# Softmax pass's node stage of a graph network: early gathers of run ends, no mask product, one product moved to the second node stage

## The reference

```python
# layer 0: softmax aggregation          N = 6250 nodes, E = 100000 edges
m = relu(feat[src]) + 1e-7
ex = exp(m - segment_max(m, dst)[dst])
msg = segment_sum(ex / segment_sum(ex, dst)[dst] * m, dst)
x = layernorm(x + (x + msg) @ W + b)
# layer 1: messages over edges (mlp: relu(h @ W + b), then normalised over all rows)
node_feat = mlp(x, W_node, ...); edge_feat = mlp(edge_attr, W_edge, ...)
message = mlp(concat([x[src], x[dst], edge_feat]), W_msg, ...)
x = layernorm(x + segment_sum(message, dst) + node_feat)
# layers 2 and 3: two mean-aggregating convolutions each, relu or elu between
```

## Time and profile before

| | us |
|---|---|
| time, median of 3 runs | 4437.25 (4429.48 to 4437.64) |
| profiled execution, span | 5171.8 |
| PE busy in it | 3159.9 (61%) |
| DVE busy | 2679.3 (52%) |
| POOL busy | 2510.8 (49%) |
| ACT busy | 1560.3 (30%) |

### The profile page before, as it was taken

One profiled execution on the slowest core, in us unless ns is written; L12 is line 12 of the kernel. 1 busy time (PEld: TensorE's weight loads), 2 busy tenths in 40 slices (PEclk: granted clock), 3 DMA queues, 4 the chain that ended last, 5 costly groups with the idle time before them and its releaser, 6 DMA issues.

```text
span 5171.8 us, 61853 instructions
## 1 busy us (share of the span) xinstructions
PE 3159.9 (61%) x18737; PEld 2317.1 (45%) x18737; DVE 2679.3 (52%) x5868; ACT 1560.3 (30%) x3684; POOL 2510.8 (49%) x2587
## 2 busy tenths in 40 slices
PE   1555555554755555555555554111159999999999
PEld 0333333333534344344344333100047777788777
DVE  4888888888645555555555556300001254433333
ACT  1777777776222222222222222100000011111000
POOL 7666666664666666666666666777720000000000
PEclk9999999999986667667667666555579999999999
DMA  5555555555134444444444443100037666666776
GB/s 183 192 198 191 195 194 194 192 192 164 56 98 111 112 121 111 116 117 111 114 118 112 111 118 85 58 0 0 13 126 282 215 218 245 247 248 251 259 276 228
DMA packets 387596, 797.88 MB, mean 154 GB/s; under 512 B 207412, under 2 KB 264600, under 8 KB 361128
## 3 DMA queue, kind: packets, MB, share of 16 engines
q1 hardware_dynamic: 239330, 586.35, 33.9%
q0 software_dynamic: 82320, 90.28, 7.9%
q10 hardware_dynamic: 65718, 118.62, 6.2%
HBM read 581.03 MB, written 213.92 MB: 154 GB/s over the span
## 4 chain that ended last, share of the span: by engine, by line
PE 25%; issue 23%; SPq 19%; DVE 3%; another core or an unknown queue 1%; DMA 0%; ACTq 0%; ACT 0%; DVEq 0%; POOL 0%
PE ps L1181 18%; SPq L626 14%; PE ps L1111 6%; SPq L601 1%; SPq L596 1%; SPq L622 1%; SPq L607 1%; SPq L617 1%; PE ps L1064 1%; ACTq L64 0%; DMA area<-adj 0%; PE ps L1083 0%; PE ps L1056 0%; DVE second L1650 0%
## 5 line engine op out<-in xcount | busy, mean ns | idle before, releaser
L770 POOL DMA_INDIRECT area<-src_table,early x784 | 752.5, 960 | 469.6 <-remote 225.5
L770 POOL DMA_INDIRECT area<-relu_table,early x784 | 739.6, 943 | 421.3 <-issue 212.4
L953 PE MATMUL ps<-ident,area 96*128 96x96 f32 x2352 | 441.4, 356 | 804.3 <-issue 555.4
L953 PEld LDWEIGHTS ps<-ident,area 96*128 96x128 f32 x2352 | 355.2, 213 | 939.2 <-issue 782.4
L1181 PE MATMUL ps<-second,area 128*128 128x288 bf16 x5194 | 652.1, 286 | 0.2 <-DVE second L1823 0.2
L1682 DVE TENSOR_TENSOR_SCAN area<-flags,area,ps 96x512 f32<-96x512 int8 x196 | 250.0, 1276 | 647.6 <-issue 552.0
L1181 PEld LDWEIGHTS ps<-second,area 128*128 128x128 f16 x5194 | 509.0, 98 | 128.5 <-DVE second L1823 0.5
L1650 DVE SCALAR_TENSOR_TENSOR second<-second,area,ps 128x512 bf16<-128x512 f32 x784 | 538.1, 741 | 0.0
L857 POOL DMA_INDIRECT adj<-out_ring x390 | 395.5, 1014 | 127.8 <-issue 127.8
L781 POOL DMA_INDIRECT adj<-copies_ring,cell_ring x392 | 388.6, 991 | 125.6 <-issue 118.9
L1111 PE MATMUL ps<-early,area 128*128 128x288 bf16 x2401 | 322.0, 292 | 204.9 <-issue 204.9
(11 more groups left out here) (330 smaller groups left out, 4709.0 us busy)
## 6 DMA issues: line engine op xcount, KB each, us to landing
area<-adj SPq DMA_DIRECT2D x147, 1632.0 KB
area<-adj SPq DMA_DIRECT2D x55, 1568.0 KB
adj<-early SPq DMA_DIRECT2D x102, 816.0 KB
soft_sums<-out_ring ACTq DMA_DIRECT2D x196, 384.0 KB
second<-key_dram SPq DMA_DIRECT2D x98, 512.0 KB
area<-dst_table SPq DMA_DIRECT2D x784, 48.0 KB
sums<-out_ring ACTq DMA_DIRECT2D x196, 192.0 KB
second<-caps_dram SPq DMA_DIRECT2D x98, 192.0 KB
```

The source lines that it names most:

```text
L770: pool.indirect_dma_start(out=src_rows[:, s, c, :], out_offset=None, in_=gather_table[p], in_offset=bass.IndirectOffsetOnAxis(ap=src_cols[ ...
L953: last = nc.tensor.transpose(ps[:, b, c * F:(c + 1) * F], r[:, (s * CH + c) * P:(s * CH + c + 1) * P], ident[0:F, 0:F])
```

## The change

POOL gathers run ends of groups 0 to 4 (FIRST_ENDS = 5, as many as fit in `area` behind the rings of the edge pass) right after its last gather of `relu_table`. Each of these groups waits for `first_ends_stored`, which SP signals after its last load of the softmax pass, when as many rounds of sums are stored as `group_stored` names for the group. Groups 5 and 6 are gathered after the last sums. Neither mask product is left: `end_row` of a node without edges now points at an extra row behind `soft_sums` and `sums`, and the product with `has` goes from POOL's L825 and from `join` (L1800). SP writes those rows, and zeros over the last three rounds of `soft_sums` (12 stores), before its wait for `later_stored`.

PE's steps in the softmax node stage are taken apart and put in another order; W_node's product, its Relu and Square move into the message node stage, ahead of the joins. `node_feat` holds the turned result in the meantime. The buffer of destination rows becomes five. DVE's `cells_of_edges`, and with it PE's turns and SP's stores of keys, move behind the node stage. Coefficients and constants of the message pass move ahead of DVE's and ACT's wait for the tables, and POOL waits for `src_table` alone. The loops over groups are written out.

The diff, cut to its core:

```diff
+        RINGS_END = RING * CH * F + 2 * RING * TE
+        FIRST_ENDS = (area.shape[1] - RINGS_END) // (GT * 2 * F)
+        def soft_ends(g):
+            at = RINGS_END + g * GT * 2 * F if g < FIRST_ENDS else (g - FIRST_ENDS) * GT * 2 * F
+            return area[:, at:at + GT * 2 * F].rearrange("p (k f) -> p k f", f=2 * F)
...
# SP, setup
+            sp.dma_start(soft_sums_all[EP:EP + 1, 0:F], ones[0:1, 0:F]).then_inc(later_stored, 16)
+            sp.dma_start(soft_sums_all[EP:EP + 1, F:2 * F], s_row[0:1, :]).then_inc(later_stored, 16)
+            sp.dma_start(sums_all[EP:EP + 1, :], s_row[0:1, :]).then_inc(later_stored, 16)
...
+                    for t in range(ET - RING * LAST_ROUNDS, ET):
+                        sp.dma_start(soft_sums_t[t], zeros.bitcast(f32)[:, 0:CH * 2 * F]).then_inc(later_stored, 16)
                     sp.wait_ge(later_stored, 16 * LATER_STORES)
                     sp.wait_ge(deg_made, 1)
                     sp.dma_start(node_cols, node_cols_in).then_inc(cells_in_landed, 16)
...
# SP, after the last load of the softmax pass
+                    for g in range(FIRST_ENDS):
+                        stored = nc.values_load(group_stored[0:1, g:g + 1], engines=[mybir.EngineType.SP], min_val=16,
+                                                max_val=16 * EI)
+                        for s in range(RING):
+                            sp.wait_ge(sums_stored[s], stored)
+                        sp.sem_inc(first_ends_stored, 1)
+                    for g in range(NG):
+                        store(g)
                     sp.wait_ge(keys_kept, 1)
...
# POOL
                 pool.wait_ge(index_made, 1)
+                if kind == SOFT:
+                    for g in range(FIRST_ENDS):
+                        pool.wait_ge(first_ends_stored, g + 1)
+                        gather_ends(g)
                 for s in range(RING):
                     pool.wait_ge(sums_stored[s], 16 * EI * (p + 1))
-                for g in range(NG):
-                    for k in range(g * GT, (g + 1) * GT):
...
-                    if g:
-                        ends_of(g - 1)
-                ends_of(NG - 1)
+                for g in range(FIRST_ENDS if kind == SOFT else 0, NG):
+                    gather_ends(g)
...
# PE, message node stage
+                    for g in range(NG):
+                        wait(pe, n["nh_kept"], g - 1)
+                        for c, w in ((0, 512), (512, GC - 512)):
+                            last = nc.tensor.matmul(features_bank(g)[:, c:c + w], W["W_node"][:, :],
+                                                    node_feat[:, g * GC + c:g * GC + c + w], start=True, stop=True)
+                        last.then_inc(n["nh_made"], 1)
...
# PE, softmax node stage
-                    over_groups(pe, turn_nodes, mix, project_nodes, late=True)
+                    turn_nodes(0)
+                    mix(0)
+                    for g in range(NG):
+                        if g + 1 < NG:
+                            turn_nodes(g + 1)
+                        if g:
+                            project_destinations(g - 1)
+                        if g + 1 < NG:
+                            mix(g + 1)
+                        turn_normed(g)
+                        project_sources(g)
+                    project_destinations(NG - 1)
...
# ACT, before storing the sums of tile s in round u
+                        if u == EI - LAST_ROUNDS and s == 0:
+                            act.wait_ge(later_stored, 16 * LATER_STORES)
...
# DVE, setup
+            chain.do(v.scalar_tensor_tensor(end_row[:, :], end_row[:, :], float(-EP), has[:, :], ALU.add, ALU.mult))
+            chain.do(v.tensor_scalar(end_row[:, :], end_row[:, :], float(EP), None, ALU.add))
...
# DVE, ahead of the joins
+                    dve.wait_ge(n["nh_squared"], NG)
+                    norm_coefs(3, nd_sum[:, :], nd_sq[:, :], n_nodes, col["g_node"], col["beta_node"], s_nd, t_nd)
+                    dve.sem_inc(coefs_made, 1)
...
# DVE, join
-                    chain.do(v.tensor_tensor(res, ends[:, bass.ds(g * GT, GT), 0:F], every(has, g), ALU.mult))
-                    chain.do(v.tensor_tensor(res, res, by_feature(s_row), ALU.mult))
+                    chain.do(v.tensor_tensor(res, ends[:, g * GT:(g + 1) * GT, 0:F], by_feature(s_row), ALU.mult))
...
# DVE, softmax node stage (cells_of_edges stood ahead of it)
-                    over_groups(dve, soft_prepare, add_and_norm, None, chain, 2 + 5)
+                    soft_prepare(0)
+                    for g in range(NG):
+                        if g + 1 < NG:
+                            soft_prepare(g + 1)
+                        add_and_norm(g)
+                    cells_of_edges()
```

More of the change, by code:

```diff
@@ L29 @@
 HC = 8
+DST_BUFS = 5
+LAST_ROUNDS = 3
 PARTS = 3
@@ L761, in _ @@
                 e, n = edge[p], node[p]
-                if p == 0:
+                if kind == SOFT:
                     pool.wait_ge(soft_stored, 16 * SOFT_STORES)
-                wait_for_tables(pool, p)
+                else:
+                    pool.wait_ge(node[p - 1]["stored"], 16 * NG)
                 def gather_chunks(t, chunks):
@@ L815, in _, with gather_ends @@
                             in_=one_h[:, :], in_offset=None).then_inc(joint_ones_made, 16)
-                def ends_of(g):
-                    groups = p * len(range(g % 2, NG, 2)) + g // 2 + 1
-                    pool.wait_ge(ends_landed[g % 2], 16 * GT * groups)
+                def gather_ends(g):
                     if kind == SOFT:
[L822 to L825, removed]
-                    else:
-                        pool.sem_inc(ends_ready, 1)
+                        rows, table = soft_ends(g), soft_sums_all
+                    else:
+                        rows, table = ends[:, g * GT:(g + 1) * GT, 0:F], sums_all
+                    wait_for_ends(pool, p, g - 2)
+                    for k in range(GT):
+                        at = end_row[:, g * GT + k:g * GT + k + 1]
+                        pool.indirect_dma_start(out=rows[:, k, :], out_offset=None, in_=table,
+                                                in_offset=bass.IndirectOffsetOnAxis(ap=at, axis=0))\
+                            .then_inc(ends_landed[g % 2], 16)
@@ L1810, in _ @@
                 if kind == SOFT:
-                    over_groups(dve, soft_prepare, add_and_norm, None, chain, 2 + 5)
-                else:
-                    over_groups(dve, nothing, join, None, chain, 5 + 5)
+                    soft_prepare(0)
+                    for g in range(NG):
+                        if g + 1 < NG:
+                            soft_prepare(g + 1)
+                        add_and_norm(g)
+                    cells_of_edges()
+                else:
+                    for g in range(NG):
+                        join(g)
             def split(source, y, done, count):
```

175 lines of the change are left out of this document (92 added, 83 removed).

## The result

The changed kernel takes 4367.47 us (median of 4 runs, 4365.22 to 4368.39) against 4437.44 before: a ratio of 0.9842, 95% interval 0.9828 to 0.9856, or 70 us less. The forecast was 4378, the range 4360 to 4402. Five more runs on another occasion gave 4364.63, ratio 0.9834 (0.9821 to 0.9848).

A forecast was written before the change was run, and what follows sets the result against it. The prediction took the softmax node stage, a chain of seven groups with no engine full, as standing alone on the path. Its terms, −26.8 − 34.8 − 2.2 − 2.5 + 6 + 0.8 + 0 = −59.5, gave 4378 us, range 4360 to 4402.

The forecast's parts named there:

- Early gathers and cells moved: Softmax stage's front: DVE goes from its last scan straight to group 0, first copy at 1278.7 against 1305.55: −26.8 us.
- Rival B: Front of the softmax node stage: the gathers are not early, 18.3 us of gain lost, 4396 us; chance 6%.
- PE's new order: Middle of the softmax node stage: copies of groups 0 to 6 span 73.7 us against 108.5: −34.8 us.
- PE still sets the pace: Softmax node stage: PE needs 13.8 us a group, DVE's own work only 12.3, so PE bounds the groups.
- 13 to 15: Sign in the changed profile: L1317 copies 13 to 15 us apart from the third on; 17 would refute.
- Tail: Softmax stage's end: last group loses W_node's 3.0 us, gains a wait for project_destinations: −2.2 us, bounds −3 and 0.
- the three terms: Softmax node stage's front, middle and end: −26.8, −34.8 and −2.2 us.
- Keys behind the node stage: Softmax stage's end: moved cells and key stores end at 1387.6, 1.2 us ahead of the tables, costing nothing.
- Start: Kernel's start: 4.7 MB of zeros take 11.7 us beside the search gathers; +6 us, bounds 0 and +11.7.
- Late scatters begin earlier: Message node stage: POOL's 2.83 us wait before the late scatters is gone: −2.5 us, bounds −2.8 and 0.
- Message node stage: W_node's product before the joins adds 17 us there, costed at 0 because late scatters end last; bounds 0 and +17.
- The stretch: Profiled span 734 us over the median, placed in message pass and late stretch; saved microseconds carried over unscaled.

The follow-up runs named there:

- second profile of before: The unchanged kernel before the change, profiled again: measured 4436.76 us, span 4435.0 us.
- the hold of 23 us: Changed kernel with DVE held by 28 memsets in front of the first join of the message node stage: 4366.90 us.
- the first profile: The kernel before the change, as profiled for the prediction: span 5171.8 us, unprofiled median 4437.25 us.
- two holds: Changed kernel with DVE held ahead of the first softmax group: 4373.73 us; with POOL held between run-end gathers and destination scatters: 4374.20 us.

## Why the prediction was right, point by point

- *Early gathers and cells moved* (−26.8): right. The copy stands 9.1 us behind the last scan's end, 8.9 forecast. Rival B's price was 18.3; undoing it cost 21.9.
- *PE's new order* (−34.8): the copies of groups 0 and 6 are 66.8 us apart, −41.8. The step that failed is "PE still sets the pace" at 13.8: PE's fourteen passes of L1037 took 3.31 us in some groups and 1.73 in others, and every other group PE waits for DVE (1.70 us at 1125.0), whose 12.04 set it. The copies are 10.9 to 13.2 apart from the third on, 12.1 on average, where 13 to 15 was to show the forecast. It lay at the bound that the prediction gave, 12.3 a group.
- *Tail* (−2.2): wrong, and it is the step that matters. From the copy of group 6 the tables land after 45.6 us and not 36.4 (1150.92 to 1196.5). The prediction counted POOL's scatters as following ACT, and never added up POOL's own list: 64 us of gathers and 68 of scatters back to back from 1063 end at 1195, as long as the groups keep ahead of it. What was won in the middle beyond the forecast, 7 us, was lost here, and the sum of the three terms, −63.8, met −62.9 measured between the last table gather and the first src_table gather. That a sum along the chain met the end of POOL's list is luck.
- *The buffers of destination rows* had no term. In the second profile of before, ACT waits 4.4 us for the one buffer inside the time that the prediction took for PE's pace; with one buffer the changed kernel is 12 to 15 us slower.
- *Keys behind the node stage* at no cost: right; SP's seven stores of them start at 1180.7 and are all issued by 1183.9, ahead of the tables at 1196.5.
- *Start* (+6): wrong, 0. The first scan moved from 96.9 to 99.65, but POOL's table gathers run from 84.3 to 1061.8 in both, and they set the pass's pace. Three times the zeros cost nothing either.
- *Late scatters begin earlier* (−2.5): right; the wait behind the last gather of sums went from 2.6 us to 0.3. But the gathers of message sums took some 9 us less as well, which had no term: the joins now start behind W_node's product, so fewer of their products stand beside POOL's gathers (22 long instructions before, 7 after). Then 7.2 came back in the late scatters, beside which the joins now run (21 long ones in place of 12).
- *Message node stage* at no cost: right, by the hold of 23 us.
- The constants moved ahead of the wait for tables had no term; the message pass lost 4.8 us, of which the shorter gathers of src_table are about 3. The kernel before without mask products, where the constants stand as they did, lost 4.5 of it too, so nothing here shows a gain from the constants.
- *The stretch* of the first profile was taken to lie in the message pass and the late scatters. Against the second profile it is 195 us up to the first run-end gather, 234 in the message pass, 15 in the late scatters and 292 behind them. From the first run-end gather to the first src_table gather both have 175, and so it did no harm to carry the microseconds over unscaled.

The range was met, but the mechanism is only half right. At the front it is as forecast. At the back the end is set by POOL's list, which the prediction did not have, and two errors of about 7 us in the stage cancel. The last 10 us are the start that cost nothing (7), the gathers of sums less what came back in the late scatters (2) and the message pass (5), less 3 lost behind the last late scatter. The move of the cells and PE's new order were not undone by themselves.

## What to carry to other kernels

Add up the list of each engine across a stage before calling it a chain: an engine that shows some 77% busy with the same gap behind each instruction, as POOL does here, can be full, and then only fewer or shorter instructions or an earlier start on that engine move the end. Read from the trace how long a hold really was before its cost is compared with a forecast: two holds here were 18.0 us for 14 and 7.3 for 9. A trace whose span is far from the measured time should be taken again before durations are summed; its stretched stages hid here that POOL was full in the passes. Where two parts of a change act on one wait, undo each on its own: the second buffer alone was worth 12 to 15 us and the other three nothing.

## What the runs showed of the hardware that was not expected

A product on DVE with both inputs in SBUF can lengthen a DMA instruction on POOL beside it, from about 0.95 us to as much as 1.6. In the changed kernel:

```profile
1093.85 0.86 DVE L1826 TENSOR_TENSOR second<-second,rstd 128x672 f32<-128x672 f32 x1
1093.94 1.58 POOL L861 DMA_INDIRECT area<-soft_sums,end_row  x1 [0.30 <-issue]
1095.83 0.95 POOL L861 DMA_INDIRECT area<-soft_sums,end_row  x1 [0.31 <-issue]
```

Replacing 25 such products by memsets took 8.0 us off 49 gathers and about 4 off the time. In POOL's list of the softmax node stage, 49 gathers and 49 scatters, such lengthening comes to an estimated 8 us (102.2 us busy, against 94.1 at 0.95 and 0.97 apiece).

The kernel before shows the other direction: DVE's products of 0.86 us took up to 2.7 where one of POOL's mask products ran beside them, four of them in the stage; without the mask products none took more than 0.9.

```profile
1120.44 2.65 DVE L1768 TENSOR_TENSOR second<-second,mean 128x672 f32<-128x672 f32 x1
1121.04 1.32 POOL L825 TENSOR_TENSOR area<-area,has 128x672 f32<-128x672 f32 x1
```

The Trainium skill, "SBUF — State Buffer", section "Who interferes with whom", states that a DVE instruction with two SBUF inputs contends with a GpSimd instruction that reads SBUF; the 2.65 us agree. It also reports a probe in which such a product did not stall a DMA of GpSimd's; for indirect DMAs the 8.0 us speak against that. Not every such product lengthens one, and what decides it was not tried.

Also open is why PE's passes took 3.31 us in some groups and 1.73 in others. The granted clock of 10 us windows is 1.00 (its level of 2.4 GHz) from 1085 to 1115, where they took 3.31, and 0.50 (1.2 GHz) from 1125 to 1135, where they took 3.19; in the window between, at 0.96, with PE 73% busy, are some of 1.73.

```profile
1085.14 3.31 PE L1037 MATMUL ps<-m_W,second 97*128 97x96 f32 x14 [1.00 <-ACT second L1364]
1117.99 1.73 PE L1037 MATMUL ps<-m_W,second 97*128 97x96 f32 x14
1129.40 3.19 PE L1037 MATMUL ps<-m_W,second 97*128 97x96 f32 x14
```
